# The second feed-forward product of four pairs of row tiles by seven half products (Strassen)

## What is computed

```
def _quant_weight(w):
    s = jnp.clip(jnp.mean(jnp.abs(w)), EPS, None)
    return jnp.clip(jnp.round(w / s), -1.0, 1.0) * s
def _quant_act(x):
    scale = 127.0 / jnp.clip(jnp.max(jnp.abs(x), axis=-1, keepdims=True), EPS, None)
    return jnp.clip(jnp.round(x * scale), -128.0, 127.0) / scale
h = gelu(_quant_act(layernorm(x)) @ _quant_weight(w1).T)     # 1250 x 4096
x = x + _quant_act(h) @ _quant_weight(w2).T                  # 1250 x 1024
```

## Time and profile before

| | |
|---|---|
| Median of 3 runs | 1041.07 us (1040.65 to 1042.8) |
| Profiled execution | 1039.78 us |
| Its span, first to last instruction | 1037.9 us |
| Mean granted TensorE clock | 0.982 |
| TensorE busy | 972.9 us (94%) |
| VectorE busy | 706.1 us (68%) |
| ScalarE busy | 434.2 us (42%) |
| GpSimd busy | 126.8 us (12%) |
| Last stage (feed-forward) | 754.2 us to the end |
| First product, 640 matmuls (L1291) | 139.9 us |
| Second product, 576 of 640 matmuls (L1320) | 126.4 us |

### The profile page before, as it was taken

One profiled execution on the slowest core, in us unless ns is written; L12 is line 12 of the kernel. 1 busy time (PEld: TensorE's weight loads), 2 busy tenths in 40 slices (PEclk: granted clock), 3 DMA queues, 4 the chain that ended last, 5 costly groups with the idle time before them and its releaser, 6 DMA issues.

```text
span 1037.9 us, 17348 instructions
## 1 busy us (share of the span) xinstructions
PE 972.9 (94%) x6781; PEld 534.8 (52%) x6781; DVE 706.1 (68%) x1038; ACT 434.2 (42%) x541; POOL 126.8 (12%) x139
## 2 busy tenths in 40 slices
PE   1799799997899999999979999999999999999998
PEld 0688655553555666555534444455544444444444
DVE  7999888877655556667779773777776555565441
ACT  5444446553355655667432120667533111222221
POOL 6300042330211110000033300010100000000000
PEclk9999899999799999999989999999999999999999
DMA  3800025664788988887455856799413554544431
GB/s 113 257 2 2 2 82 213 233 244 169 251 305 320 342 321 311 316 312 274 161 168 155 213 125 203 266 375 349 160 28 81 122 122 111 121 107 108 108 93 36
DMA packets 166144, 188.90 MB, mean 182 GB/s; under 512 B 126520, under 2 KB 126842, under 8 KB 161984
## 3 DMA queue, kind: packets, MB, share of 16 engines
q1 hardware_dynamic: 159679, 165.47, 49.8%
q0 software_dynamic: 6400, 22.55, 6.7%
HBM read 137.98 MB, written 35.33 MB: 167 GB/s over the span
## 4 chain that ended last, share of the span: by engine, by line
PE 83%; DVE 9%; issue 3%; DMA 2%; ACT 1%; another core or an unknown queue 0%; DVEq 0%; SPq 0%; ACTq 0%
PE ps L1093 20%; PE ps L1291 13%; PE ps L1320 12%; PE ps L1273 8%; PE ps L1200 7%; PE ps L1216 7%; PE ps L1157 2%; DMA abs_e<-in_L_ffn_w 2%; PE ps L1026 2%; PE ps L1061 1%; PE ps L980 1%; DVE o_key L1840 1%; PE ps L953 1%; PE ps L971 1%; DVE w1l L2097 1%
## 5 line engine op out<-in xcount | busy, mean ns | idle before, releaser
L1291 PE MATMUL ps<-w1q,xqt 128*128 128x512 fp8e4 x640 | 139.9, 379 | 0.6 <-issue 0.6
L1642 ACT ACTIVATE hf<-ps,fs 128x512 f32<-128x512 f32 x80 | 54.9, 687 | 183.2 <-PE ps L1291 183.2
L1320 PE MATMUL ps<-w2q,hqt 128*128 128x512 fp8e4 x576 | 126.4, 379 | 0.0
L2347 DVE TENSOR_REDUCE hm<-hf 128x1 f32<-128x512 f32 x80 | 54.2, 684 | 74.0 <-ACT hf L1642 74.0
L1291 PEld LDWEIGHTS ps<-w1q,xqt 128*128 128x128 f16 x640 | 62.4, 98 | 76.0 <-issue 1.1
L1320 PEld LDWEIGHTS ps<-w2q,hqt 128*128 128x128 f16 x576 | 56.3, 98 | 66.9
L1093 PE MATMUL ps<-wt_h,xt 128*128 128x512 f16 x320 | 85.3, 379 | 0.0
L1093 PE MATMUL ps<-gwt_h,xt 128*128 128x512 f16 x320 | 84.7, 379 | 0.3 <-issue 0.2
L1200 PE MATMUL ps<-xdh,w1h 128*128 128x314 f16 x256 | 76.3, 298 | 4.4 <-DVE w1l L2097 2.7
L1200 PE MATMUL ps<-xdh,w1l 128*128 128x314 f16 x256 | 75.8, 296 | 0.0
L1200 PE MATMUL ps<-xdl,w1h 128*128 128x314 f16 x256 | 75.6, 295 | 0.0
(11 more groups left out here) (317 smaller groups left out, 1850.7 us busy)
## 6 DMA issues: line engine op xcount, KB each, us to landing
wstage<-in_L_ffn_w SPq DMA_DIRECT2D x32, 1024.0 KB, 8.9
abs_in<-in_L_ffn_w SPq DMA_DIRECT2D x18, 1024.0 KB, 6.7
abs_e<-in_L_ffn_w SPq DMA_DIRECT2D x14, 1024.0 KB, 5.6
fnat_b<-in_L_ffn_w SPq DMA_DIRECT2D x28, 512.0 KB, 7.4
fnat_a<-in_L_ffn_w SPq DMA_DIRECT2D x27, 512.0 KB, 5.6
eo_d<-eo SPq DMA_DIRECT2D x16, 512.0 KB, 3.0
hq_d<-hq SPq DMA_DIRECT2D x8, 1024.0 KB, 6.3
xs_d<-xs_all SPq DMA_DIRECT2D x10, 512.0 KB, 2.9
```

The costliest lines, as they stand in the source:

```text
L1291: last = mm(ps[:, n % 4, :], xqt[:, u, k, :], w1q[:, k // 2, n * 512:(n + 1) * 512, k % 2], start=(k == 0), stop=(k == KD - 1))
L1320: last = mm(ps[:, 4 + h, :], hqt[:, u, k, :], w2q[:, k // 2, h * 512:(h + 1) * 512, k % 2], start=(k == 0), stop=(k == KF - 1))
L1642: cp(hf[:, i % 2, n * 512:(n + 1) * 512], ps[:, n % 4, :], ACT.Gelu, scale=fs[:, i % 2, 3:4]).then_inc(s_ge, 1)
L2347: last = v.tensor_reduce(hm[:, u, n:n + 1], hf[:, u, n * 512:(n + 1) * 512], AX.X, ALU.max, apply_absolute_value=True)
```

## The change

For tiles 1 to 8, in pairs (a, b) = (1, 2), (3, 4), (5, 6), (7, 8), the second product is made in Strassen's way. Of the transposed hidden values of a and b two halves each are taken (hidden rows 0 to 2047 and 2048 to 4095: a1, a2, b1, b2), of the first half of them and of the weights blocks w11, w12, w21, w22. Seven half products of 16 matmuls each (`FACTORS`) take the place of eight. They need sums:

- of weights, by GpSimd, once: t3 = w22 - w12, t2 = t3 + w11, w12 - w11 (in place), t4 = w21 - t2; and w12 restored at the end, for tile 9. Each is 8192 fp8 elements per partition, all small whole numbers.
- of values, by VectorE, per pair: s1 = b1 + b2, b1 = a1 - b1, a1 = s1 - a1, a2 = a2 - a1, each 128 by 2048 in float16, `hqt` in place but for s1.
- of results, by VectorE: nine updates or sums of 128 by 512 and one of 128 by 1024 per pair, which add PSUM banks, or the sum `shared`, times the row's scale (now kept per tile in `hscale`) into x. ScalarE copies the first half product into `shared`.

The results go to memory from x; `out_t` is gone. The order changes too: TensorE does both first products of a pair's next two tiles, then seven half products. VectorE's and the queue's programs are laid out in pairs to match.

```
+            pool.wait_ge(s_fc, 4 + 64)
+            pool.wait_ge(s_agg, NT)
+            g.tensor_tensor(t3[:, :, :, :], wq22, wq12, ALU.subtract, saturate=False).then_inc(s_wsum, 1)
+            pool.wait_ge(s_wsum, 1)
+            g.tensor_tensor(t2[:, :, :, :], t3[:, :, :, :], wq11, ALU.add, saturate=False).then_inc(s_wsum, 1)
+            pool.wait_ge(s_f2, 1)
+            g.tensor_tensor(wq12, wq12, wq11, ALU.subtract, saturate=False).then_inc(s_wsum, 1)
+            pool.wait_ge(s_wsum, 3)
+            g.tensor_tensor(t4[:, :, :, :], wq21, t2[:, :, :, :], ALU.subtract, saturate=False).then_inc(s_wsum, 1)
+
+            pool.wait_ge(s_pair, done(PAIRS - 1, 5))
+            g.tensor_tensor(wq12, wq12, wq11, ALU.add, saturate=False).then_inc(s_wsum, 1)
...
+        PAIRS = (NT - 2) // 2
+        ORDER = (1, 2, 5, 6, 4, 7, 3)
+        ORDER_END = (1, 5, 2, 6, 4, 7, 3)
...
+            half = KF // 2
+            FACTORS = {1: (hqt[:, 1, 0:half, :], wq11, 4), 2: (hqt[:, 1, half:KF, :], wq21, 5), 5: (s1, wq12, 6),
+                       6: (hqt[:, 1, 0:half, :], t2, 7), 4: (hqt[:, 0, half:KF, :], t4, 4),
+                       7: (hqt[:, 0, 0:half, :], t3, 5), 3: (hqt[:, 1, half:KF, :], wq22, 6)}
+
+            def pair_waits(p, m):
+
+                if m == 1:
+                    pe.wait_ge(s_hqt, 32 * p + 16)
+                    pe.wait_ge(s_pairread, 1 + 10 * p)
+                elif m == 5:
+                    pe.wait_ge(s_wsum, 3)
+                    pe.wait_ge(s_rsum, 4 * p + 1)
+                elif m == 6:
+                    pe.wait_ge(s_rsum, 4 * p + 3)
+                elif m == 4:
+                    pe.wait_ge(s_wsum, 4)
+                    pe.wait_ge(s_first, p + 1)
+                elif m == 7:
+                    pe.wait_ge(s_pairread, 1 + 10 * p + 2)
+                elif m == 3:
+                    pe.wait_ge(s_pairread, 1 + 10 * p + 4)
+                    pe.wait_ge(s_rsum, 4 * p + 4)
...
+                    for k in range(half):
+                        last = mm(ps[:, bank, :], a[:, k, :], b[:, k // 2, :, k % 2], start=(k == 0), stop=(k == half - 1))
+                    last.then_inc(s_pair, 1)
+                    if end and m in (4, 7):
+                        pe.wait_ge(s_hq, 2 + NT)
+                        hidden_t(0 if m == 4 else 1, 3)
...
             ffn_in(0, 0)
             ffn_in(1, 1, first=True)
-            ffn_out(0, 0, turned=0)
-            with pe.Fori(0, NT // 2 - 2) as j:
+            ffn_out(0)
+            pe.wait_ge(s_f2r, 1)
+            with pe.Fori(0, PAIRS - 1) as p:
                 for u in range(2):
-                    ffn_in(2 * j + 2 + u, u)
-                    ffn_out(2 * j + 1 + u, 1 - u)
-            ffn_in(NT - 2, 0)
-            ffn_out(NT - 3, 1)
-            ffn_in(NT - 1, 1)
-            ffn_out(NT - 2, 0, ahead=True)
+                    ffn_in(2 * p + 2 + u, u)
+                ffn_pair(p, ORDER)
+            for u in range(2):
+                ffn_in(NT - 2 + u, u)
+            ffn_pair(PAIRS - 1, ORDER_END, end=True)
             last_out()
```

The queue keeps the order within a tile (write hq, input of a later tile, load hqt) and puts the results of a pair together; of the loop over pairs p:

```
+                if more:
+                    hidden_rows(2 * p + 3)
+                    input_t(2 * p + 5)
+                    hidden_t(2 * p + 3)
+                result(2 * p + 1)
+                result(2 * p + 2)
+                if more:
+                    hidden_rows(2 * p + 4)
+                    if 2 * p + 6 < NT:
+                        input_t(2 * p + 6)
+                    hidden_t(2 * p + 4)
```

More of the change, by code:

```diff
@@ L754, in result @@
                         sp.wait_ge(s_f2r, i + h + 1)
-                        sp.dma_start(out[(NT - 1) * P:N, cols], out_t[0:LAST, u, cols]).then_inc(s_out[u], 16)
+                        sp.dma_start(out[(NT - 1) * P:N, cols], x[0:LAST, i, cols]).then_inc(s_out, 16)
                 else:
                     sp.wait_ge(s_f2r, i + 1)
-                    sp.dma_start(res[i], out_t[:, u, :]).then_inc(s_out[u], 16)
+                    sp.dma_start(res[i], x[:, i, :]).then_inc(s_out, 16)
             for i in range(3):
                 input_t(i)
[L762 to L769, removed]
+            hidden_rows(1)
+            input_t(3)
+            hidden_t(1)
+            result(0)
+            hidden_rows(2)
+            input_t(4)
+            hidden_t(2)
+            for p in range(PAIRS):
+                more = p + 1 < PAIRS
+                if more:
[9 more added lines that the diff above has]
+                    hidden_t(2 * p + 4)
+            result(NT - 1)
             for u in range(2):
@@ new lines, in ffn_pair @@
+            def ffn_pair(p, order, end=False):
+                for m in order:
+                    pair_waits(p, m)
+                    hold(pe)
+                    a, b, bank = FACTORS[m]
+                    for k in range(half):
[4 more added lines that the diff above has]
+                        hidden_t(0 if m == 4 else 1, 3)
@@ L1329, in last_out @@
                     if 1 <= q <= 2:
[L1330 removed]
+                        hidden_t(q + 1, 3)
                     for k in range(8 * q, 8 * q + 8):
[L1332 removed]
+                        last = mm(ps[:, 0, :], hqt_end[:, k, :], w2q[:, k // 2, 0:512, k % 2], start=(k == 0), stop=(k == KF - 1))
                 last.then_inc(s_f2, 1)
[L1334 to L1335 removed]
+                for k in list(range(half, KF)) + list(range(half)):
+                    if k == 0:
+                        pe.wait_ge(s_wsum, 5)
+                    last = mm(ps[:, 1, :], hqt_end[:, k, :], w2q[:, k // 2, 512:D, k % 2], start=(k == half), stop=(k == half - 1))
                 last.then_inc(s_f2, 1)
@@ L1679, in _ @@
             dve.sem_inc(s_hq, 2)
+            dve.sem_inc(s_pairread, 1)
             v.memset(nat_i[:, 2, :], 2047).then_inc(s_pad, 1)
```

165 lines of the change are left out of this document (114 added, 51 removed).

## The result

The changed kernel takes 1099.03 us (median of 4 runs, 1098.34 to 1100.86). The kernel before, timed beside it, takes 1041.93 us (4 runs, 1040.65 to 1043.28). The ratio is 1.0548, with a 95% interval of 1.0516 to 1.058. The forecast was 1108 us, in a range of 1048 to 1130. The profiled execution took 1099.68 us, with a span of 1098.0 us against 1037.9 and a mean granted clock of 0.956 against 0.982. So 60.1 us of span have to be found. TensorE is busy for 974.3 us (972.9 before), VectorE for 785.2 (706.1), GpSimd for 201.0 (126.8).

The account below looks back on a forecast made before the run. TensorE alone was taken to bound the last stage. -13.8 + 13.5 + 4.2 + 1.5 + 20.7 + 17.5 + 14.6 + 8.5 = +66.7 on 1039.78 gave 1106.5, and 1.3 for the median 1108 us; range 1048 to 1130.

Parts of the forecast that it names:

- A sum's length: GpSimd's five weight sums: 17.5 us each, scaled from its float32 sum of 128x1024 in 2.352 us.
- five for one: Whole forecast: five microseconds follow each microsecond of a GpSimd sum; 15 to 18.8 us gives 1095 to 1115.
- Tile 0: First two sums hold back the first tile's scaling by 24.1 us; +20.7 on TensorE, inside tile 1's first product.
- First pair: Before m = 5: third and fourth sums delay tile 2's scaling, +17.5, besides the 4.5 us wait for s1.
- Pairs 2 and 3: TensorE waits 4.5 us in each before m = 5, for s1 from the later tile's hqt.
- Last pair: m = 5 comes second there and waits for s1: +4.2.
- Result wait: Before the loop, TensorE waits for VectorE to read the first tile's result: +1.5.
- Last tile: Fifth sum holds VectorE before the last tile's rounded rows, which TensorE wants to transpose: +14.6.
- The clock: TensorE at half clock after waits: 5.1 for three long ones, 3.4 for four short ones, together +8.5.
- Not held through: Rival: VectorE is not locked out for a whole GpSimd sum, or sums are short; 1051 us, chance 0.16.
- Double cost: Rival: fp8 elements cost GpSimd double, 35 us per sum; 1195 us, chance 0.12.
- The third: Rival: later tile's hqt lands 4.5 us sooner and the lock is absent; 1030 us, chance 0.05.

Follow-up runs that it names:

- one wait: The changed kernel with GpSimd's fourth sum held until VectorE has rounded the input of tile 4: 1089.19 us.
- fill blocks: Three column blocks of the next tile's first product put ahead of the half product needing s1, against the changed kernel without GpSimd sums: 1039.53 us.

## Why the prediction was right

**Right in kind and nearly in size.** The forecast rested on two overlaps of 1.5 and 2.4 us and said that the same holds for a sum of 15 us or more. It does: four VectorE operations end with a sum or behind it, and leaving the sums out takes 42.6 us away. The Trainium skill, page "SBUF — State Buffer", section "Who interferes with whom", gives the same rule; the trace agrees at 14.8 us.

- **-13.8 us** for 64 matmuls: the page of the profile counts 6717 matmuls for 6781. Right.
- **A sum's length.** 17.5 us predicted from a float32 row, 14.75 measured, just under the floor of 15 that I gave. An fp8 element costs 1.80 ns (14.75 us for 8192) where float32 had 2.11: from pieces of 512 (1.09 us) and 1024 elements (2.00 us) it is 1.78 ns and 0.18 us fixed. The estimate from the Trainium skill, page "GPSIMD Engine Reference", section "Elementwise — side-by-side cycle accounting", was 18.0 us and would have erred to the same side. By my own five for one, 13.8 us too many.
- **Tile 0:** 20.7 predicted, 14.8 measured. With 2.75 us less on each of two sums, 20.7 - 5.5 = 15.2. The one-element product ended with the first sum and the scaling did find the second one begun, as said.
- **First pair:** 17.5 + 4.5 predicted, 16.4 measured. Two sums of 14.8 in place of 17.5 take 5.5 off, which gives 16.5.
- **Pairs 2 and 3:** 9.0 predicted, 4.60 + 4.96 measured. **Last pair:** 4.2 and 3.91. **Result wait:** 1.5 and 1.95.
- **Last tile:** 14.6 predicted, 11.8 measured, again one sum's 2.75.
- **The clock:** 8.5 predicted, 12.7 measured. This was the term that was too small by most (pairs 2 and 3 were by 0.6, the result wait by 0.45). A wait of 4 to 5 us cost 1.6 to 2.1 us (I had taken 0 to 1.7, and its middle), a long one 1.85 to 2.75 (I had 1.7, from a stretch that was soon at the full clock again).
- Not in the sum: the stage began 1.75 us later, and other runs show it begin between 754 and 759 us whatever was changed in it. It is scatter of the work ahead of it.

The errors partly cancel: the terms of the sums were 14.3 us too high, the clock, the start and the small terms nearly 8 too low. That the total came this close is in part luck. What is left is 6.6 us of span; with the 1.3 that I added for the median, and the medians' own scatter, the forecast was 9 us too high.

**The rivals.** "Not held through" is out: leaving the sums out gives 1056 us, near that rival's 1051, and the kernel with them is 43 us above. Double cost is out by the five rows. The third, that without lock and with hqt sooner it would be faster (1030 us), had its place right but not its size or its cause. The later tile's hqt did not land sooner by itself; without sums it does when the queue's two lines are swapped, and the kernel takes 1039.0, not 1030, since the last pair's wait (3.86 us and 1.7 at the half clock) and those at the result (1.79) and the last tile (1.42) stay. With fill blocks in place of the swap, with the last pair's and the result's waits nearly gone, and with 16 matmuls more, it is 1034.7. I had seen that the queue's order makes hqt late, and took it as given; without sums, swapping it is free.

## What to carry to other kernels

Before giving an idle GpSimd work, look at what VectorE does at that time, not at how long it is idle: 73.8 us of GpSimd cost 43 us on a path that TensorE bounded. The price falls by placing the work beside maxima or PSUM reads (one wait, 9.8 us) and by cutting it up, but pieces one behind the other still take most of a piece from every VectorE scaling, rounding and operation with two inputs from SBUF; their length and their start have to be chosen together. And look at who waits in a queue ahead of a load that has become urgent: without sums, swapping two transfers was worth 17 us.

## What the runs showed that I had not expected

- Beside pieces that follow at once on each other, the two engines take turns, one instruction each. Beside pieces of 1.09 us the 2.35 us scaling takes 2.95, beside pieces of 2.00 us 3.87; a GpSimd piece of 1.09 us lasts up to 3.15 when VectorE is scaling. But between the third and the fourth whole sum, 0.08 us apart, no VectorE operation was waiting, and the one that came 2.9 us later waited for all the rest, 11.9 us.
- A wait of TensorE need not cost clock. After 2.65 us of wait the 16 matmuls took 3.61 us and the granted clock stayed at 1.00; after 3.30 us in one kernel nothing was lost, and after 3.35 us in another the granted clock was 0.50 from 818 to 820 and 64 matmuls took 15.66 us instead of 13.98.
